# Retention denominators: VectorE's reciprocal replaced by ScalarE's exponential of the negative logarithm

## The reference

```python
def step(carry, xs):
    S, K = carry
    pq, pk, vt, bt, mt = xs
    K = K * bt[..., None] + pk[:, :, None, :]
    S = S * bt[..., None, None] + pk[:, :, None, :, None] * vt[:, :, None, None, :]
    num = jnp.einsum('bhd,bhmdc->bhmc', pq, S)
    den = jnp.einsum('bhd,bhmd->bhm', pq, K) + EPS
    y = jnp.sum(num / den[..., None] * mt[..., None], axis=2)
    return ((S, K), y)
```

## Time and profile before

| | us |
|---|---|
| median of 3 timed runs | 2272.37 |
| lowest and highest of them | 2271.41, 2273.75 |
| the profiled execution, its own time | 2265.08 |
| its span in the profile | 2263.4 |
| the retention stage in it, about | 803 to 1092 |

### The profile page before, as it was taken

One profiled execution on the slowest core, in us unless ns is written; L12 is line 12 of the kernel. 1 busy time (PEld: TensorE's weight loads), 2 busy tenths in 40 slices (PEclk: granted clock), 3 DMA queues, 4 the chain that ended last, 5 costly groups with the idle time before them and its releaser, 6 DMA issues. The chain is left out here.

```text
span 2263.4 us, 35922 instructions
## 1 busy us (share of the span) xinstructions
PE 1980.8 (88%) x12434; PEld 1484.5 (66%) x12434; DVE 1702.2 (75%) x5243; ACT 1016.5 (45%) x1596; POOL 498.3 (22%) x560
## 2 busy tenths in 40 slices
PE   5786799987999867754699978999999999979999
PEld 3554699976999823322699965566556555549998
DVE  6997788865888769999588876766766766628887
ACT  3442244433444333322344444566665665554443
POOL 1110100012000023221100014534533544230000
PEclk8998899998999987776799989999999999989999
DMA  3000100000000000000000000000000000000000
GB/s 97 6 5 4 54 1 1 1 1 1 1 1 2 13 27 1 0 1 0 1 1 1 1 1 1 1 1 1 1 1 1 1 1 1 1 1 6 11 11 15
DMA packets 17638, 15.75 MB, mean 7 GB/s; under 512 B 4209, under 2 KB 16177, under 8 KB 16946
## 3 DMA queue, kind: packets, MB, share of 16 engines
q1 hardware_dynamic: 15152, 12.66, 1.8%
q10 hardware_dynamic: 2306, 0.78, 0.2%
HBM read 10.55 MB, written 2.88 MB: 6 GB/s over the span
## 5 line engine op out<-in xcount | busy, mean ns | idle before, releaser
L2256 DVE TENSOR_REDUCE soft_mx<-psum 128x1 f32<-128x512 f32 (+3 forms) x608 | 380.4, 659 | 198.5 <-PE psum L2127 111.9
L2173 ACT ACTIVATE soft_prob<-psum 128x1024 f32<-128x1024 f32 (+3 forms) x384 | 305.1, 813 | 209.8 <-PE psum L2054 208.9
L2123 PE MATMUL psum<-soft_own,soft_stack 128*128 128x512 f32 (+3 forms) x768 | 250.4, 376 | 18.9 <-DVE soft_mx L2256 16.5
L2054 PE MATMUL psum<-soft_stack,soft_own 128*128 128x512 f32 (+3 forms) x768 | 228.4, 381 | 2.9 <-POOL soft_stack L2029 2.2
L2054 PEld LDWEIGHTS psum<-soft_stack,soft_own 128*128 128x128 f32 x768 | 121.2, 189 | 134.1 <-issue 74.7
L2123 PEld LDWEIGHTS psum<-soft_own,soft_stack 128*128 128x128 f32 x768 | 139.2, 191 | 77.7 <-DVE soft_mx L2256 63.1
L2071 PE MATMUL psum<-soft_prob,soft_v_pad 128*32 128x512 f32 (+3 forms) x1536 | 163.9, 498 | 3.5 <-ACT soft_prob L2173 2.1
L1056 DVE SCALAR_TENSOR_TENSOR x<-psum,ffn1b_cw,x 128x128 f32<-128x128 f32 x512 | 144.0, 343 | 30.1 <-PE psum L934 21.3
L1056 DVE SCALAR_TENSOR_TENSOR x<-psum,ffn0b_cw,x 128x128 f32<-128x128 f32 x512 | 144.1, 343 | 29.9 <-PE psum L934 21.5
L1056 DVE SCALAR_TENSOR_TENSOR x<-psum,ffn1a_cw,x 128x128 f32<-128x128 f32 x512 | 144.1, 344 | 29.8 <-PE psum L934 21.0
L1056 DVE SCALAR_TENSOR_TENSOR x<-psum,ffn0a_cw,x 128x128 f32<-128x128 f32 x512 | 144.1, 344 | 29.5 <-PE psum L934 21.0
(11 more groups left out here) (435 smaller groups left out, 3845.4 us busy)
## 6 DMA issues: line engine op xcount, KB each, us to landing
s_ffn_w<-in_ffn_w SPq DMA_DIRECT2D x4, 1024.0 KB, 8.3
out_x<-x SPq DMA_DIRECT2D x8, 256.0 KB, 2.3
x<-in_x SPq DMA_DIRECT2D x4, 384.0 KB, 7.4
mamba_coef_dram<-mamba_out_coef SPq DMA_DIRECT2D x8, 96.0 KB, 1.6
s_ret_w<-in_ret_w SPq DMA_DIRECT2D x1, 640.0 KB, 3.5
x<-in_x SPq DMA_DIRECT2D x4, 128.0 KB, 3.9
s_ret_cos<-in_ret_cos SPq DMA_DIRECT2D x1, 512.0 KB, 4.9
s_ret_sin<-in_ret_sin SPq DMA_DIRECT2D x1, 512.0 KB, 5.5
```

Source lines behind the costliest of these rows:

```text
L2054: ins = pe.matmul(e_ps[:, n % 2, j, low(n):BLK], own[:, u % 3, 2 * pair + j, kt * P:(kt + 1) * P], stack[:, u % HT, qb * BLK + low(n):(qb ...
L2123: ins = pe.matmul(per_head[:, n, :], stack[:, u % HT, i * P:(i + 1) * P], own[:, u % 3, g, half * BLK:half * BLK + width], start=(n == 0), ...
L2173: nc.scalar.activation(prob[:, done % PROBS, :, low(n):BLK], e_ps[:, n % 2, :, low(n):BLK], ACT.Exp, scale=float(HD) ** -0.5).then_inc(exp ...
L2256: nc.vector.tensor_reduce(mx[:, i, half, heads.start:heads.stop], bank[:, 0:width * len(heads)].rearrange("p (g k) -> p g k", k=width), AX ...
```

## The change

The copy of the denominators becomes a natural logarithm of the same input (den + 1e-6). A second activation on ScalarE waits for it and writes exp(-1 x rd) into the same tile, which is 1 / (den + 1e-6); it now signals `inverted`. VectorE's reciprocal and its wait for `den_copied` are gone. `den_copied`, for which TensorE also waits before it overwrites the sums, is now signalled by the logarithm.

```diff
@@ -1616,7 +1616,9 @@
                 act.wait_ge(den_ready, DECAYS * (q + 1))
                 if q:
                     act.wait_ge(spread_ready, DECAYS * q)
-                nc.scalar.activation(rd[:, :, :], den_ps, ACT.Identity, bias=eps[:, :]).then_inc(den_copied, 1)
+                nc.scalar.activation(rd[:, :, :], den_ps, ACT.Ln, bias=eps[:, :]).then_inc(den_copied, 1)
+                act.wait_ge(den_copied, q + 1)
+                nc.scalar.activation(rd[:, :, :], rd[:, :, :], ACT.Exp, scale=-1.0).then_inc(inverted, 1)
 
@@ -1715,8 +1717,6 @@
             def invert(q):
-                dve.wait_ge(den_copied, q + 1)
-                nc.vector.reciprocal(rd[:, :, :], rd[:, :, :]).then_inc(inverted, 1)
                 dve.wait_ge(inverted, q + 1)
                 dve.wait_ge(mix_ready, q + 1)
                 nc.vector.tensor_tensor(rd[:, :, :], rd[:, :, :], mix[:, q % 2, :, :], ALU.mult).then_inc(rd_ready, 1)
```

## The result

The changed kernel took 2256.62 us (median of 4 runs, 2254.73 to 2258.16), the kernel before 2271.89 (4 runs, 2267.61 to 2273.75). The ratio is 0.9936 with a 95% interval of 0.9922 to 0.9950: 11 to 18 us less. The forecast was 2261.6 with a range from 2257.5 on.

A forecast was written before the change was run, and what follows sets the result against it. VectorE was taken to bound the retention stage's steady part; block gains of 7.3 us (five blocks), 1.64, 1.74 and 0.13 sum to 10.8, so 2272.37 - 10.8 = 2261.6 us, with a range of 2257.5 to 2269.0.

The forecast's parts named there:

- the first load: ScalarE, each block, ahead of the wait for the denominators' sums: runs in 7.7 us idle (3.35 in block 7), costs nothing.
- the second: Table load between logarithm and exponential: path of 2.29 us, exponential done 0.61 us before VectorE is free in block 2.
- late next: TensorE: Spread matmuls cannot start before the numerators' sums end: gain 1.46 us in five blocks, 1.64, 1.74 and 0.13 in others.
- the ceiling of the gain: VectorE: eight removed reciprocals of 1.744 us, 14.0 us in all, taken as the most the change could gain.
- The first, a switch at twice the row: ScalarE's table load takes 2.57 us instead of 1.28: gain only 7.1 us, time 2265.3; chance 0.20.
- The second, gain turned into slowed scans: One more scan in each of six blocks runs at 2.36 us instead of 1.21: gain 3.9, time 2268.5; chance 0.10.
- The third: Both loads on ScalarE's path, each at twice the row: chain 6.1 us, loss 13 us, time 2285.6; chance 0.08.
- its limit of 3.5 us: Loads on the path above 3.5 us mean a loss: mean distance now 4.46 us, logarithm, exponential and signals take 1.0.

The follow-up runs named there:

- the kernel with more loads: Changed kernel plus a one-column exponential and logarithm per block between logarithm and exponential, so three table loads on the path: 2277.30 us, ratio 1.0033 against the kernel before.
- the second comparison: The changed kernel again, unedited, against the kernel before: 2257.26 us against 2268.86, ratio 0.9947.
- the filled versions: Changed kernel with four unread matmuls between the second decay's denominator and numerator sums, 2256.34 us; with ten more ahead of these sums, 2254.89 us.

## Why the prediction was right or wrong

**The mechanism held.** VectorE bounded the stage; the first load ran in ScalarE's idle time; the second was covered by `products` and `finish`; TensorE was the next one to be late, and its idle time ahead of the spread fell from 11.5 to 0.3 us (0.7 by the forecast). Seven of eight products started with no wait, and block 0's waited 0.81 us (some 0.7 by the sum; 0.58 in the two other traces). The path from the logarithm's start to the exponential's end was 2.21 us in block 2, for 2.29 with the signals in the sum.

**The term that failed is "late next: TensorE".** I moved the spread to the end of TensorE's sums and kept its 3.78 us in every block, and the output matmuls of block 7 as they were. I had written down that the idle 1.5 us ahead of the spread would vanish, and did not ask what that does to the clock of the work behind it. VectorE's idle time by the forecast and as measured:

| us | before | forecast | after |
|---|---|---|---|
| wait for the spreads, L1728 | 10.4 | 12.8 | 9.8 |
| wait for block 7's output matmuls, L1735 | 3.7 | 3.7 | 2.6 |
| wait for the exponential, L1722 | 0 | 0.7 | 0.8 |

The first two rows miss 4.1 us, and that is nearly all of the difference in the stage, 15.0 us for 10.8. The two have different standing:

- The wait for the spreads (3.0 us) goes with the closed gap. In the kernel before, filling it brought them from 30.2 us in all to 17.5 and 23.5, and shortened the stage by 4.5 us with six matmuls and 5.5 with three (the timed runs by 3.6 and 2.5, with intervals of 2 to 6 and 0.5 to 4.5). With the change in place and the gap open, in the kernel with more loads, they took 29.6 us. With the reciprocal gone, the gap closed and no loads, they took 27.1.
- The wait for block 7's output matmuls (1.1 us) goes with the granted clock, 1.00 for 0.56, but is not shown to come from the gap: these matmuls took 2.05 us with the reciprocal kept and the gap at 1.51 us too. Why the clock rose earlier there stays open.

By blocks, from one start of L1619 to the next, the gain was 1.2 us in block 0 (forecast 0.13; its spread took 2.77 us), 1.6 to 1.9 in blocks 1 to 3 (1.46), 2.05 in block 4 (1.64), 1.6 in blocks 5 and 6 (1.74 and 1.46), and 3.9 in block 7 (1.46), where nothing on VectorE covers either the spread or the output matmuls. In block 0 the clock is not all of it: without the reciprocal and without loads its spread took 3.78 us, and the block gained 1.3 us all the same. Ahead of block 0's logarithm the changed kernel lost 0.56 us, 0.3 of it in a wait of `rope` for the ring's matmuls; in its other two traces it lost 0.0 and 0.1.

**The ceiling was wrong by the same step.** That VectorE's 14.0 us are "the ceiling of the gain" holds only while the other engines keep their durations. The stage gained 15.0, 15.6 and 15.4 us in three traces, so the lower end of the range lay too high. By how much the timed runs passed it is chance: 2256.62 is 0.9 us under 2257.5, less than the spread of the four runs, and against a gain of 11.6, as in the second comparison, the same range would have held. The miss that counts is that of the stage, 15 us for 10.8.

**The rivals.** The first, a switch at twice the row, is out: 1.30 us each time, alone and three in a row. So is the drain of some 1380 ns a switch that the Trainium skill states in "ScalarE: Activation LUTs", section "What ACT_TABLE_LOAD costs": the trace agrees with its 1283 ns, and shows 0.02 us before and after the load. The second, gain turned into slowed scans, did not happen in the changed kernel (101.0 us of scans for 100.7), and may show in small in the filled versions (102.7). The third did not happen either, for the first load did not wait for the sums; but its arithmetic held in the kernel with more loads, where 3.85 us of loads and 0.4 of short activations on the path made a loss, as its limit of 3.5 us says.

**Time outside the stage stays open.** In three comparisons the medians differ by 15.3, 11.6 and 13.9 us, the stage by some 15.4. All three traces of the changed kernel have a softmax stage of 698.6 to 698.8 us; the two of the kernel before have 693.8 and 697.9. Among the other kernels, none of which touches that stage, it goes from 692.4 to 698.6 us. Whether the shift of that stage in time costs the changed kernel something there, or these are draws of the clock, was not settled.

## What to carry to other kernels

When an engine's own work shrinks, ask of the next engine not only when it starts but at which clock it will run: more or less idle time on TensorE ahead of a stretch of matmuls can change their duration (a spread of 3.78 us took between 2.6 and 3.8 in the changed kernel). Table loads in an engine's idle time cost nothing here; count only those between the event that is waited for and its consumer, at 1.3 us each. And where an unrelated stage of the program varies by 4 us, compare the lengths of the touched stage, not the spans.

## What was not expected of the hardware

The granted clock answered to TensorE's work with a delay. With three filling matmuls it was still 1.00 in block 1's sums (1.07 us), right after 1.78 us of idle time, and 0.53 on average in the matmuls that followed them without a gap (0.52 us each), and in the changed kernel three of eight spreads without a gap ahead still took 3.78 us. What raised it in nearly all blocks was work put well ahead of the stretch that matters: with ten matmuls before the second decay's sums, blocks 1 to 5 had spreads of 2.05 us in all three such traces. What exactly the chip looks at was not tried, and block 7's output matmuls show that it is more than the gap. The Trainium skill says in "TensorE: Matmul & The Clock Gate", section "HAM oscillation — how this bites in real kernels", that matmuls in short bursts with waits between them can fall back to the low clock in every burst; the traces agree in that the fourteen spreads behind an idle 1.5 us or more in the kernel before all ran at the low clock, and in that matmuls that nobody reads, put into that idle time, took 4.5 and 5.5 us off the stage.
